# Cross-attention on one Trainium2 core: heads projected undivided, the softmax division on the projected rows, the two projections at tiles 5 and 9

## The reference, cut to what matters

```python
def _L0_xattn_ref(x, context, w_q, w_kv, w_out, b_out):   # x (4, 512, 256), context (4, 1601, 256)
    HEADS, DIM_HEAD = 16, 64
    q = (x @ w_q).reshape(b, n, HEADS, DIM_HEAD)
    kv = (context @ w_kv).reshape(b, m, 2, HEADS, DIM_HEAD)
    k, v = (kv[:, :, 0], kv[:, :, 1])
    attn = jnp.einsum('bnhd,bmhd->bhnm', q, k) * scale
    attn = jax.nn.softmax(attn, axis=-1)
    out = jnp.einsum('bhnm,bmhd->bnhd', attn, v).reshape(b, n, INNER)
    return out @ w_out + b_out
x = _layernorm(x + _L0_xattn_ref(x, ctx_1024, ...), axis=-1)
```

## Time and profile before

| | |
|---|---|
| median of three runs | 2048.67 us (2048.62 to 2049.02) |
| profiled execution | 2053.94 us, its span 2052.2 us |
| blocks of the cross-attention | from 282 us to 1763 us of the span |
| TensorE busy | 1746.8 us (85%) |
| VectorE busy | 1191.0 us (58%) |
| ScalarE busy | 832.0 us (41%) |
| GpSimd busy | 1323.0 us (64%) |
| mean granted clock of TensorE | 0.919 |

### The profile page before, as it was taken

How to read it: one execution, slowest core, us unless ns; L and a number is a source line. 1 busy time by engine, 2 the same in 40 slices (tenths; PEclk the granted TensorE clock), 3 DMA queues, 4 the chain that set the end, 5 groups by cost and what they waited for, 6 DMA issues and landing times. The chain is left out here.

```text
span 2052.2 us, 32755 instructions
## 1 busy us (share of the span) xinstructions
PE 1746.8 (85%) x10682; PEld 1212.3 (59%) x10682; DVE 1191.0 (58%) x2046; ACT 832.0 (41%) x1228; POOL 1323.0 (64%) x711
## 2 busy tenths in 40 slices
PE   7553599999989999998999999899999998509990
PEld 5443466666656666665666666566666664408980
DVE  4788555556565656556565665655565654553345
ACT  3111234444444444444444444444444444224440
POOL 2988338577676667576776676675766677454544
PEclk8775689999999999999999999999999999559995
DMA  5000200000200000010000001000000000321223
GB/s 185 1 21 24 79 1 22 1 22 0 73 1 22 22 3 22 0 52 22 21 1 23 1 21 52 21 22 1 21 1 21 15 1 1 124 84 63 71 63 128
DMA packets 37813, 68.09 MB, mean 33 GB/s; under 512 B 3560, under 2 KB 27504, under 8 KB 36656
## 3 DMA queue, kind: packets, MB, share of 16 engines
q1 hardware_dynamic: 33936, 56.12, 8.1%
q0 software_dynamic: 3744, 10.23, 1.5%
HBM read 52.84 MB, written 13.50 MB: 32 GB/s over the span
## 5 line engine op out<-in xcount | busy, mean ns | idle before, releaser
L1001 POOL TENSOR_TENSOR xa_total<-xa_total,xa_pexp 128x1024 f32<-128x1024 f32 (+1 forms) x352 | 852.9, 2423 | 52.7 <-ACT xa_pexp L942 27.3
L1060 DVE TENSOR_REDUCE xa_parts<-ps_ring 128x1 f32<-128x402 f32 x1024 | 532.3, 565 | 299.8 <-PE ps_ring L887 292.8
L942 ACT ACTIVATE xa_pexp<-ps_s 128x1024 f32<-128x1024 f32 (+1 forms) x416 | 422.7, 1025 | 419.0 <-PE ps_s L842 391.9
L856 PE MATMUL ps_pv<-xa_pexp,xa_v 128*64 128x512 f32 (+1 forms) x1664 | 399.8, 604 | 0.0
L887 PE MATMUL ps_ring<-xa_k_hi,xa_q_hi 64*128 64x402 f32 x1024 | 235.0, 377 | 32.7 <-DVE xa_parts L1060 31.4
L856 PEld LDWEIGHTS ps_pv<-xa_pexp,xa_v 128*64 128x64 f32 (+1 forms) x1664 | 106.2, 137 | 181.9 <-issue 148.3
L887 PEld LDWEIGHTS ps_ring<-xa_k_hi,xa_q_hi 64*128 64x128 f32 x1024 | 142.7, 186 | 118.2 <-DVE xa_parts L1060 58.9
L1001 POOL TENSOR_TENSOR xa_total<-xa_pexp 128x1024 f32<-128x1024 f32 x32 | 76.3, 2384 | 190.9 <-ACT xa_pexp L942 189.6
L1048 DVE TENSOR_TENSOR xa_k_lo<-ps_ring,xa_k_hi 128x402 fp32r<-128x402 f32 (+1 forms) x128 | 73.6, 575 | 214.7 <-ACT xa_k_hi L953 214.7
L842 PE MATMUL ps_s<-xa_q_hi,xa_k_hi 64*128 64x512 f32 (+1 forms) x832 | 194.0, 433 | 3.6 <-DVE xa_k_lo L1048 2.8
L842 PE MATMUL ps_s<-xa_q_neg,xa_row_one 64*128 64x512 f32 (+1 forms) x832 | 174.4, 393 | 0.0
(11 more groups left out here) (263 smaller groups left out, 2946.2 us busy)
## 6 DMA issues: line engine op xcount, KB each, us to landing
wa_raw<-in_pack_a SPq DMA_DIRECT2D x17, 768.0 KB, 4.4
ex_w_raw<-in_pack_e SPq DMA_DIRECT2D x8, 1026.0 KB, 5.3
ctx_raw<-in_ctxT SPq DMA_DIRECT2D x4, 1601.0 KB, 8.5
wb_raw<-in_pack_b SPq DMA_DIRECT2D x16, 256.0 KB, 2.6
ex_w_hi<-ybuf SPq DMA_DIRECT2D x8, 512.0 KB, 7.6
sa_xT<-in_xT SPq DMA_DIRECT2D x8, 256.0 KB, 6.4
X<-in_x SPq DMA_DIRECT2D x1, 2048.0 KB, 11.5
x_hi<-sa_x1s_hi SPq DMA_DIRECT2D x16, 128.0 KB, 2.1
```

Of the source, the lines that this page charges most:

```text
L856: ins = nc.tensor.matmul(ps_pv[half(h), :], v[0:m, t, at:at + XD], pexp[0:m, buf, h, :], start=t == 0, stop=t == MT - 1)
L942: nc.scalar.activation(pexp[0:m, buf], ps_s[0:m, (p * MT + t) % 2], ACT.Exp, scale=XD ** -0.5)\
L1001: nc.gpsimd.tensor_tensor(total[p][0:m], first, pexp[0:m, buf], ALU.add).then_inc(s["add_done"], 1)
L1060: nc.vector.tensor_reduce(parts[:, h, q, c:c + 1], ps_ring[:, r, 0:CW], AX.X, ALU.max)\
```

## The change

- RS: `total` becomes the stationary operand, in eight pieces of 128 queries, and a single column of ones moves. The sums then lie with the queries on the partitions, eight numbers in each, as the projected rows do. VectorE takes their reciprocals, 128x8, into `inv`; ScalarE's copy and R1 to R3 are gone.
- ScalarE makes `att_hi` straight from `ps_pv`, R4 makes `att_lo` from `ps_pv` at tile 0, and the next block's first PV waits for it (`att_ready`).
- OP: the heads can't be summed before the division, so each is projected by itself: for each j, 12 matmuls of 64 rows write head 0 to one bank and head 1 to another. VectorE adds each to X multiplied by the reciprocal of its row: four scaled additions of 128x256 for each j, those of the second head behind those of the first.
- j = 0 stands behind the PV of tile 5, j = 1 behind those of tile 9. `project_out()` gives both steps of a j; the first takes its bank and waits, the second issues the matmuls.

```diff
 def chain(p, back):
-    return {3: ([("RS", p)], []), 4: ([], [("R1", p, 0)]), 5: ([], [("R1", p, 1)]), 6: ([], [("R1", p, 2)]),
-            7: ([], [("R1", p, 3), ("R2", p)]), 8: ([], [("R3", p), ("R4", p)]),
-            9: ([], [("OP", p, 0, back), ("OP", p, 1, back)])}
+    return {0: ([], [("R4", p)]), 3: ([("RS", p)], []), 5: ([], project_out(p, 0, back)), 9: ([], project_out(p, 1, back))}
+
+def project_out(p, j, back):
+    return [("OP", p, j, h, back) for h in range(2)]
...
     if last:
-        end = [("RS", 1)] + [("R1", 1, k) for k in range(4)] + [("R2", 1), ("R3", 1), ("R4", 1),
-                                                               ("OP", 1, 0, 0), ("OP", 1, 1, 0)]
+        end = [("R4", 1), ("RS", 1)] + project_out(1, 0, 0) + project_out(1, 1, 0)
...
-        pv_sb, sums, inv, att = (sb(x, [P, N]) for x in ("pv_sb", "sums", "inv", "att"))
+        row_raw, inv = sb("row_raw", [P, P]), sb("inv", [P, 2, 2, NC])
... TensorE
                     if t == 0:
-                        need(pe, s["pv_copied"], n.of("COPY"))
+                        need(pe, s["att_ready"], n.of("COPY"))
...
                     for h in range(2):
-                        ins = nc.tensor.matmul(ps_ring[half(h), r, :], ones[:, 0:XD], total[p][:, h, :],
-                                               start=True, stop=True)
+                        for q in range(NC):
+                            at = h * NC + q
+                            ins = nc.tensor.matmul(ps_ring[:, r, at:at + 1], total[p][:, h, q * P:(q + 1) * P], ones[:, 0:1],
+                                                   start=True, stop=True)
...
                 elif kind == "OP":
-                    p, j = st[1:3]
+                    p, j, h, back = st[1:]
                     r = take_bank(n)
-                    pe.wait_ge(s["att_ready"], n.of("R4"))
+                    if h == 0:
+                        pe.wait_ge(s["att_ready"], n.of("R4"))
+                        return
+                    banks = (n.job(("OP", p, j, 0, back))[0], r)
                     for q in range(2):
                         cs = slice((2 * j + q) * P, (2 * j + q + 1) * P)
-                        terms = [(att_hi[:, cs], w_out(wa_hi, p)), (att_lo[:, cs], w_out(wa_hi, p)),
-                                 (att_hi[:, cs], w_out(wa_lo, p))]
-                        ins = project(ps_ring[:, r, q * E:(q + 1) * E], terms)
-                    ins.then_inc(filled[r], 1)
+                        for k, (x, w) in enumerate(((att_hi, wa_hi), (att_lo, wa_hi), (att_hi, wa_lo))):
+                            for g in range(2):
+                                ins = nc.tensor.matmul(ps_ring[:, banks[g], q * E:(q + 1) * E], x[half(g), cs], w_out(w, p)[half(g)],
+                                                       start=k == 0, stop=k == 2)
+                                if q == 1 and k == 2:
+                                    ins.then_inc(filled[banks[g]], 1)
... ScalarE
                     act.wait_ge(s["pv_done"], n.of("PV") + 1)
-                    need(act, s["att_done"], n.of("R2"))
-                    nc.scalar.copy(pv_sb[:], ps_pv[:]).then_inc(s["pv_copied"], 1)
+                    nc.scalar.copy(att_hi[:], ps_pv[:]).then_inc(s["att_hi_done"], 1)
... VectorE
+                elif kind == "RS":
+                    r = n.slot()
+                    dve.wait_ge(filled[r], n.of("ring%d" % r) + 1)
+                    nc.vector.reciprocal(inv[:, st[1]].rearrange("p h q -> p (h q)"), ps_ring[:, r, 0:2 * NC]).then_inc(drained[r], 1)
                 elif kind == "R4":
                     dve.wait_ge(s["att_hi_done"], n.of("R4") + 1)
-                    nc.vector.tensor_tensor(att_lo[:], att[:], att_hi[:].bitcast(F32), ALU.subtract)\
+                    nc.vector.tensor_tensor(att_lo[:], ps_pv[:], att_hi[:].bitcast(F32), ALU.subtract)\
                         .then_inc(s["att_ready"], 1)
                 elif kind == "OP":
-                    p, j, back = st[1:]
+                    p, j, h, back = st[1:]
                     r = n.slot()
                     dve.wait_ge(filled[r], n.of("ring%d" % r) + 1)
-                    xs = X[:, bass.ds((i - back) // QUADS * NC + 2 * j, 2), :].rearrange("p t e -> p (t e)")
-                    nc.vector.tensor_tensor(xs, ps_ring[:, r, :], xs, ALU.add).then_inc(drained[r], 1)
+                    seen, c = n.job(("RS", p) if h == 0 else ("OP", p, j, 0, back))
+                    dve.wait_ge(drained[seen], c)
+                    for q in range(2):
+                        xs = X[:, bass.ds((i - back) // QUADS * NC + 2 * j + q, 1), :].rearrange("p t e -> p (t e)")
+                        ins = nc.vector.scalar_tensor_tensor(out=xs, in0=ps_ring[:, r, q * E:(q + 1) * E],
+                                                             scalar=inv[:, p, h, 2 * j + q:2 * j + q + 1], in1=xs,
+                                                             op0=ALU.mult, op1=ALU.add)
+                    ins.then_inc(drained[r], 1)
```

More of the change, by code:

```diff
@@ L743, in cross_attention @@
         ps_ring = ctx.enter_context(nc.psum_tensor("ps_ring", [P, RING, 512], F32))
-        s = sems(ctx, nc, "ones_set zero_set scores_ready exp_done pv_done add_done pv_copied att_ready "
+        s = sems(ctx, nc, "ones_set zero_set scores_ready exp_done pv_done add_done att_ready "
                           "k_hi_done q_hi_done shift_ready x1_in ctx_hi_done ctx_lo_done "
-                          "wa_hi_done wa_lo_done wb_hi_done wb_lo_done att_done att_hi_done filled0 filled1 filled2 "
-                          "drained0 drained1 drained2 inv_ready")
+                          "wa_hi_done wa_lo_done wb_hi_done wb_lo_done att_hi_done filled0 filled1 filled2 "
+                          "drained0 drained1 drained2")
         s.update(loads.sems)
@@ L959, in handle @@
                     nc.scalar.copy(q_hi[p][:], ps_ring[:, r, :]).then_inc(s["q_hi_done"], 1)
[L960 to L967, removed]
                 elif kind == "SH":
@@ L1027, in _ @@
             nc.vector.memset(negmax[:], 0.0)
-            nc.vector.memset(att[:], 0.0).then_inc(s["zero_set"], 1)
+            nc.vector.memset(row_raw[:], 0.0).then_inc(s["zero_set"], 1)
             dve.wait_ge(s["zero_set"], 1)
             for h in range(2):
-                nc.vector.memset(att[h * XD:h * XD + 1, 0:P], 1.0).then_inc(s["zero_set"], 1)
+                nc.vector.memset(row_raw[h * XD:h * XD + 1], 1.0).then_inc(s["zero_set"], 1)
             dve.wait_ge(s["zero_set"], 3)
-            nc.vector.tensor_copy(row_one[:], att[:, 0:P]).then_inc(s["ones_set"], 1)
+            nc.vector.tensor_copy(row_one[:], row_raw[:]).then_inc(s["ones_set"], 1)
             def handle(i, n, st):
```

## The result

The changed kernel takes 2129.1 us (2124.1 to 2138.1 over four runs) beside 2048.9 (2048.6 to 2052.0) for the one before: ratio 1.0393 (95% interval 1.0356 to 1.0430), 80 us slower. I had forecast 2081 us, 32 us slower, with a range up to 2118: the direction and the places of the waits hold, the sum is 48 us short.

The account below looks back on a forecast made before the run. TensorE's own order was taken to set the time. Even blocks +9, odd +28.5, batch ends -5, last block +1.8, tail -2 make +32 us: 2053.9 profiled to 2086, median 5.3 lower, 2081 us; range 2050 to 2118.

Parts of the forecast that it names:

- +1.0 a block: RS on TensorE: 16 weight loads and a shape change, 1.9 us in place of 0.91.
- Clock 1.00 within the blocks: Expected sign in the profile after: TensorE's granted clock stays at full rate inside the blocks.
- rival 4: Clock falls in RS, three to four us at half clock behind each: +1.5 to 2 a block, 2135 us; chance 0.05.
- the chain: Division and projection of the pair before: 1.9 + 1.45 + 2.25 = 5.6 us a block, instead of 4.87 (even), 3.7 (odd).
- the batch ends: Three blocks: OP waits near 3.7 us for a bank, not 5.94 for `att_lo`; -1.7 us each, -5 together.
- OP's pairs: OP on TensorE: 12 concurrent pairs of 64 rows at 0.117 us, 0.70 us for each half.
- rival 5: OP's pairs of 64 rows don't overlap or are held by issue: +0.8 to 1.4 us a block, 2115; chance 0.04.
- Scaled additions: VectorE behind OP: 0.48 us each (0.42 to 0.55), a bank of two drained in 0.86 us.
- rival 3: Scaled additions wait for GpSimd: at 0.7 us mean +70, at 1.2 over +200, 2150 us and more; chance 0.06.
- S10: Score matmul of tile 10, behind the second half of OP: starts some 1.3 us behind OP's end.
- rival 2: No TensorE wait behind OP, since relieved VectorE drains both banks in time: -37 us, 2012; chance 0.09.
- Tail: Kernel's end, from GpSimd's last addition to the last scaled addition: -2 us.

Follow-up runs that it names:

- cols64: The changed kernel with 64 columns of ones moving in RS instead of one, same 16 weight loads: 2100.7 us.
- after_old_rs: The changed kernel with the old RS (two matmuls of 512 columns, ones stationary) and the new OP, division not right: 2062.1 us.
- before_both_rs: The kernel before with the eight one-column sum matmuls put in front of its own RS, which overwrites them; old OP: 2139.3 us.
- two_adds: The changed kernel with one of the two scaled additions for each bank, half of the projected rows never added to X: 2064.1 us.

## Why the prediction fell short, step by step

**The failed step: the clock behind RS, put at nothing.** The sum prices RS by its length alone, +1.0 a block, with "Clock 1.00 within the blocks". "Each RS is short and stands in dense work" was my only reason against a clock that falls in RS (rival 4), and I gave it 0.05. The runs show that rival's mechanism, with the size that it had: 3.4 us at half clock (I had 3 to 4) and 1.6 us each (1.5 to 2), behind 23 of the 31 RS where I had priced it behind all. The gate's stretch in the earlier trace rows was the row that spoke, a TensorE always busy and still at 0.50; I read it as a case of another kind. These are 37 us of the traces, and the net 30 of `cols64` (the batch ends got 5 back).

**Mis-sized terms: the chain and the batch ends.** Where no fall comes, a chain costs 6.2 us in an even block and 6.0 in an odd one, not 5.6. In an even block (4) the step from S of tile 3 to S of tile 4 is 2.12 us over block 0's, not 1.9 (16 passes of 0.117 where I had 0.111, and 0.25 for the entry where I had 0.1). The three steps behind S of tile 5 are 1.74 us over, not 1.45 (OP with its entry 0.82 for 0.70, waiting 0.92 for 0.75), and the three behind S of tile 9 are 2.36 over, not 2.25. In odd blocks without a fall (15 and 23, 52.68 us) the waiting behind tile 5 is 0.75, as forecast. 12 x 0.62 and 15 x 0.43 are 14 us. `after_old_rs` has the OP side of that by itself: +11 us where my terms sum to 0. The three batch-end blocks are together 2.3 us shorter than before, with three falls behind RS in them (5 us); without these they would be 7 shorter, where I had 5. `ctx_lo` ended 1.3 us sooner in each, for the reason shown above and in none of my terms, so that the wait for a bank is 2.38 us and not 3.7.

**What held.** OP's pairs at 0.115 us each, 0.69 for a half, against 0.70 (rival 5 is out). Scaled additions: median 0.481, four in 1.86 us; the slowest of 256 takes 0.488, though 109 of them lie wholly within an operation of GpSimd (rival 3 is out; its +70 was too high by its own figures, 256 x 0.22 are 56). The Trainium skill (SBUF — State Buffer, SBUF: two separate sides) names operations with two SBUF inputs for the lock against GpSimd; with one factor a partition as the second SBUF input no row here shows a lock. S10 1.34 us behind OP for 1.3. The relieved VectorE didn't drain in time (rival 2 is out): its busy time fell by 107 us, yet TensorE's idle time ahead of the maxima rose from 32.7 to 47.2 us, 44.1 of them for the scaled additions. Tail -2.2 for -2.

**The sum as it should have been:** 32 forecast, 37 for 23 falls, 14 for the chains, 2 less at the batch ends: 81, for 80 measured. Neither error alone would have left the range: 2081 and the net 30 of the clock are 2111, and 2081 and the other 18 are 2099; 2118 was its upper edge.

## What to carry to other kernels

Before many narrow matmuls replace a few wide ones, price their loads and then ask whether a row shows what the clock did behind such work; where it can fall, give the same loads wider moving operands, or fewer passes. Where jobs take turns in a ring of few banks, time is won by spreading the jobs that meet at one place (56 us by one table here) or by shortening the drains at that place (42 us with half of the scaled additions left out), not by taking work off the draining engine elsewhere (107 us of VectorE's here). A half-idle engine can still hold the others up: count banks held times drain time at the place, not its busy share.

## What the runs showed of the hardware

- 1.87 us of one-column float32 matmuls back to back were followed by a fall of the granted clock from 1.00 to 0.5 for 3.4 us, 23 times in 30 in the kernel after, with no gap in TensorE's records from the start of RS to the fall; in `before_both_rs` 15 times in 30, in `two_adds` 4 in 30. With 64 columns in the same 16 loads, or with 8 passes of two columns (1 us), there was none. The last block is left out of these counts: there RS stands behind a wait for GpSimd, and the PV pair behind it is slow in every kernel here. The Trainium skill (TensorE: Matmul & The Clock Gate, HAM oscillation) tells of a clock that falls when TensorE waits between bursts; here the fall comes without a wait, and the measurement decides.
- A pass with a stationary 128x128 float32 operand took 0.117 us with 1 column and 0.120 with 64 (1.87 and 1.92 us over 16).
- A VectorE subtraction with both inputs in SBUF that starts while GpSimd's addition (also from SBUF) runs ends a fixed time behind it. `ctx_lo` (128x1601) took 1.86 to 3.73 us over the fourteen traces, and at all 42 batch ends it ended 1.68 to 1.69 us behind the end of GpSimd's addition. `att_lo` before (128x512) took 0.68 us in the 13 cases where none ran, and ended 0.55 us behind it in the 19 where one did. With one input in PSUM (`att_lo` after) it took 0.68 to 0.69 us in all 32.
